# The keys' stage of a delta-rule attention: taps as diagonal matrices, blocks to lanes by DMA

## What is computed

```python
mixed = x @ W_qkv
xp = jnp.pad(mixed, ((0, 0), (KW - 1, 0), (0, 0)))
conv = sum((xp[:, i:i + Tt, :] * conv_w[:, i] for i in range(KW)))
mixed = jax.nn.silu(conv)
q, k, v = jnp.split(mixed, [KEY_DIM, 2 * KEY_DIM], axis=-1)
...
def step(S, inp):
    qt, kt, vt, gt, bt = inp
    S = S * jnp.exp(gt)[..., None, None]
    pred = jnp.einsum('bhk,bhkv->bhv', kt, S)
    u = (vt - pred) * bt[..., None]
    S = S + jnp.einsum('bhk,bhv->bhkv', kt, u)
    o = jnp.einsum('bhk,bhkv->bhv', qt, S)
    return (S, o)
```

## Time and profile before

| | us |
|---|---|
| runs timed | 5175.81, 5176.11, 5183.47, median 5176.11 |
| the profiled execution | 5175.35 |
| its span, first to last instruction | 5173.4 |
| TensorE, VectorE, ScalarE, GpSimd busy | 4783.1, 3891.6, 3016.7, 690.7 |
| keys' stage, first layer | 283.2 to 820.8 |
| keys' stage, second layer | 2819.0 to 3356.9 |

### The profile page before, as it was taken

The page is one execution under the profiler, slowest core; times in us unless marked ns, Lnnn a source line. Parts: engine busy times, 40 slices in busy tenths (PEclk is TensorE's granted clock), DMA queues, the critical chain, the costliest instruction groups (busy, mean ns, idle before and its releaser), DMA issues. The chain is left out here.

```text
span 5173.4 us, 92884 instructions
## 1 busy us (share of the span) xinstructions
PE 4783.1 (92%) x33236; PEld 4034.2 (78%) x33236; DVE 3891.6 (75%) x7782; ACT 3016.7 (58%) x9830; POOL 690.7 (13%) x740
## 2 busy tenths in 40 slices
PE   5999875999999999999969989399999999999998
PEld 3577754888888888888845877378888888888887
DVE  6837797888878878878852488877787877777876
ACT  1134544777777777777721454266666666666665
POOL 0000000221121121122100000011212111212121
PEclk7999987999999999999979999699999999999999
DMA  1022322222222222222200232222222222222222
GB/s 54 27 83 101 124 99 84 77 78 69 77 81 74 77 78 69 81 77 76 67 29 25 94 119 103 99 77 79 74 75 82 69 77 78 71 77 83 69 77 61
DMA packets 481684, 397.20 MB, mean 77 GB/s; under 512 B 302280, under 2 KB 377592, under 8 KB 480782
## 3 DMA queue, kind: packets, MB, share of 16 engines
q1 hardware_dynamic: 481230, 391.29, 25.0%
HBM read 287.79 MB, written 103.38 MB: 76 GB/s over the span
## 5 line engine op out<-in xcount | busy, mean ns | idle before, releaser
L1116 DVE SCALAR_TENSOR_TENSOR conv_l<-mix_l,taps_l,conv_l 128x512 f32<-128x512 f32 x1152 | 865.0, 751 | 271.1 <-ACT conv_l L948 243.9
L757 PE MATMUL pj_l<-x_high,w_high_l 128*128 128x512 f32 x1280 | 586.7, 458 | 159.5 <-ACT w_high_l L957 159.5
L757 PE MATMUL pj_l<-x_high,w_low_l 128*128 128x512 f32 x1280 | 512.0, 400 | 0.1
L757 PE MATMUL pj_l<-x_low,w_high_l 128*128 128x512 f32 x1280 | 512.1, 400 | 0.0
L1318 POOL TENSOR_TENSOR fac_l<-den_l,powers 128x4 f32<-128x4 f32 x256 | 257.7, 1007 | 1833.5 <-DVE den_l L1239 1830.6
L922 PE MATMUL gb_l<-wo_l,gT_l 128*128 128x256 f32 x2048 | 481.7, 384 | 0.0
L404 PE MATMUL pk_l<-x_high,wf_high_l 128*128 128x512 f32 x1024 | 425.0, 415 | 20.9 <-DVE wf_low_l L490 20.9
L1084 ACT ACTIVATE Z_l<-gb_l 128x128 f32<-128x128 f32 x1024 | 266.7, 290 | 296.9 <-PE gb_l L913 296.9
L922 PEld LDWEIGHTS gb_l<-wo_l,gT_l 128*128 128x128 f32 x2048 | 370.0, 190 | 73.9 <-ACT Z_l L1084 31.0
L1249 DVE SCALAR_TENSOR_TENSOR x<-gb_l,fac_l,x 128x256 f32<-128x256 f32 x1024 | 413.1, 476 | 10.1
L757 PEld LDWEIGHTS pj_l<-x_high,w_high_l 128*128 128x128 f32 x1280 | 241.3, 189 | 229.1 <-ACT w_high_l L957 159.8
(11 more groups left out here) (188 smaller groups left out, 10884.5 us busy)
## 6 DMA issues: line engine op xcount, KB each, us to landing
rows_l<-rows_dram SPq DMA_DIRECT2D x128, 1024.0 KB, 5.5
k_dram<-kT_l SPq DMA_DIRECT2D x128, 256.0 KB, 2.0
kk_dram<-key_kkS_l SPq DMA_DIRECT2D x128, 256.0 KB, 2.0
kq_l<-k_dram SPq DMA_DIRECT2D x128, 256.0 KB, 3.3
kkS_l<-kk_dram SPq DMA_DIRECT2D x128, 256.0 KB, 5.7
w_raw_l<-in_wx SPq DMA_DIRECT2D x32, 640.0 KB
t_dram<-lane_t_l SPq DMA_DIRECT2D x6, 1536.0 KB, 6.9
key_taps_l<-in_ktaps SPq DMA_DIRECT2D x32, 256.0 KB, 3.7
```

The source lines that it names most:

```text
L757: ins = nc.tensor.matmul(pj_bank(c, t), wt[:, k, t, :], xt[:, k, :, at], start=(k == 0 and n == 0), stop=(k == KD - 1 and n == 2))
L1116: ins = nc.vector.scalar_tensor_tensor(out, mix[:, t, :, i:i + P], wt(i), out, ALU.mult, ALU.add)
```

## The change

It rebuilds key_blocks for both layers; the other stages stay.

- TensorE projects without taps (6 products), subtracts from the sum in place the high part that ScalarE has copied out, by one product with the matrix -1, so that the low part is left (1 product), and convolves high and low parts with diagonal matrices of the taps (4 taps x 3 terms = 12 products). The four key products stay. The steps run one slot apart: project(q), subtract_high(q - 1), convolve(q - 2), products(q - 3). Sums of the projection lie in three banks pk, those of the taps in two banks pc.
- ScalarE copies the high part (keep_high) and the low part (keep_low), makes SiLU and copies the products. It makes eight 128x128 tap matrices for each head (tap_diagonals), four in each of the slots c = 2 and c = 3. Its copies into own are gone. Group work now comes six slots behind the end of a group.
- SyncE stores, besides keys and products, the diagonal blocks of each slot from kkS to own_dram, by eight DMAs of 32 x 4 x 32 elements (16 KB each), and loads them by head into lanes (load_lanes, 512 KB) once all stores of the head have landed. Taps come by one DMA at the start.
- VectorE has no folding and no transpose. It makes the low part of unfolded weights (a quarter of the size), prepares all heads of a group together, and GROUPED is (1, 2, 2, 2, 2, 2, 2, 2, 1).

The core of the diff:

```diff
-    RING = 4
-    WAITING = 5
-    GROUPED = (2, 3, 3, 3, 2, 2, 1)
+    RING = 6
+    AHEAD = 4
+    LANED = 6
+    GROUPED = (1,) + (2,) * 7 + (1,)
     MOST = max(GROUPED)
+    STORES = 1 + QUADS * GROUPS
...
+    group_of = [k for k, n in enumerate(GROUPED) for _ in range(n)]
+    behind = [CHUNKS * (last_of[k] + 1) for k in range(len(GROUPED))]
...
+        pk = ps("pk", [P, 3, WIDE])
+        pc = ps("pc", [P, 2, WIDE])
...
+                    for r in range(QUADS):
+                        rows = slice(r * QUAD, (r + 1) * QUAD)
+                        own = by4(kkS[rows, q % 2, :])[:, :, rows]
+                        for g in range(GROUPS):
+                            lane = r * QUAD + (c * GROUPS + g) * BATCH
+                            sp.dma_start(m.own_dram[L][h, lane:lane + BATCH].rearrange("b i j -> i b j"),
+                                         own).then_inc(kk_out[q % 2], 16)
+
+                def load_lanes(h):
+                    for par in range(2):
+                        sp.wait_ge(kk_out[par], 16 * STORES * (h + 1) * CHUNKS // 2)
+                    if h >= LANED:
+                        sp.wait_ge(solve, STEPS * (group_of[h - LANED] + 1))
+                    sp.dma_start(K[:, ring_of(h), :, :], m.own_dram[L][h]).then_inc(lane_in[ring_of(h)], 16)
...
+                    for k in range(1, len(GROUPED)):
+                        if q == behind[k] + 7:
+                            store_blocks(k - 1)
+                    if q < SLOTS:
+                        sp.wait_ge(k_silu, q + 1)
+                        sp.dma_start(m.k_dram[L][h, c], kT[:, q % 2, :]).then_inc(k_out[q % 2], 16)
                     if q >= 1:
                         store_products(q - 1)
+                    if q >= 1 and c == 0:
+                        load_lanes(h - 1)
...
+                    at = slice(HALO + c * P, HALO + (c + 1) * P)
+                    terms = ((wk_high, m.x_high), (wk_high, m.x_low), (wk_low, m.x_high))
+                    for k in range(KD):
+                        for n, (wt, xt) in enumerate(terms):
+                            ins = nc.tensor.matmul(pk[:, q % 3, :], wt[:, h % RING, k, :], xt[:, k, :, at],
+                                                   start=(k == 0 and n == 0), stop=(k == KD - 1 and n == 2))
+                    ins.then_inc(k_mm, 1)
...
+                    pe.wait_ge(high_ok, q + 1)
+                    nc.tensor.matmul(pk[:, q % 3, :], minus[:, :],
+                                     p_high[:, h % 2, :, HALO + c * P:HALO + (c + 1) * P], start=False, stop=True,
+                                     skip_group_check=True).then_inc(rest_mm, 1)
...
+                    pe.wait_ge(low_ok, q + 1)
+                    if c == 0:
+                        pe.wait_ge(diag_ok, 2 * TAPS * (h + 1))
+                    if q >= 2:
+                        pe.wait_ge(k_silu, q - 1)
+                    terms = ((tap_high, p_high), (tap_low, p_high), (tap_high, p_low))
+                    for i in range(TAPS):
+                        for n, (wt, pt) in enumerate(terms):
+                            ins = nc.tensor.matmul(pc[:, q % 2, :], wt[:, h % 2, i, :],
+                                                   pt[:, h % 2, :, c * P + i:(c + 1) * P + i],
+                                                   start=(i == 0 and n == 0), stop=(i == TAPS - 1 and n == 2))
+                    ins.then_inc(c_mm, 1)
...
+                for q in range(SLOTS + 3):
+                    if q < SLOTS:
+                        project(q)
+                    if 1 <= q < SLOTS + 1:
+                        subtract_high(q - 1)
+                    if 2 <= q < SLOTS + 2:
+                        convolve(q - 2)
+                    if q >= 3:
+                        products(q - 3)
...
+                    for i in some:
+                        for src, dst in ((taps_high[:, :, :].bitcast(F32), tap_high), (taps_low[:, :, :], tap_low)):
+                            nc.scalar.activation(dst[:, h % 2, i, :], eye, ACT.Copy,
+                                                 scale=src[:, h, i:i + 1]).then_inc(diag_ok, 1)
...
+                    act.wait_ge(k_mm, q + 1)
+                    if c == 0 and h >= 2:
+                        act.wait_ge(c_mm, CHUNKS * (h - 1))
+                    nc.scalar.activation(p_high[:, h % 2, :, HALO + c * P:HALO + (c + 1) * P], by4(pk[:, q % 3, :]),
+                                         ACT.Copy).then_inc(high_ok, 1)
...
+                def copy_products(q):
                     act.wait_ge(kk_mm, q + 1)
...
+                        act.wait_ge(kk_out[q % 2], 16 * STORES * (q // 2))
...
+                    if q < SLOTS:
+                        keep_high(q)
+                    if 1 <= q < SLOTS + 1:
+                        keep_low(q - 1)
+                    if 2 <= q < SLOTS + 2:
+                        silu(q - 2)
+                    if q >= 3:
+                        copy_products(q - 3)
+                    if q < AHEAD:
+                        weights_high(q + 1)
+                    if c >= 2 and h < KHEADS - 1:
+                        tap_diagonals(h + 1, range(2 * c - 4, 2 * c - 2))
+                    if q == 4:
+                        act.wait_ge(lanes_in, 16 * 2 * QUADS)
+                        spread_gains(0)
+                        spread_gains(1)
+                    for k in range(len(GROUPED) - 1):
+                        if k >= 1 and behind[k] <= q < behind[k] + GROUPED[k]:
+                            n = last_of[k - 1] + AHEAD + 1 + q - behind[k]
+                            if n < KHEADS:
+                                weights_high(n)
+                        if q == behind[k] + 6:
+                            if k >= 1:
+                                transpose_blocks(k - 1)
+                            if k + 2 < len(GROUPED):
+                                spread_gains(k + 2)
...
+                for k, size in enumerate(GROUPED):
+                    if k >= 1:
+                        for h in range(last_of[k - 1] + AHEAD + 1, min(last_of[k] + AHEAD + 1, KHEADS)):
+                            weights_low(h)
+                    for n in range(size):
+                        h = first_of[k] + n
+                        dve.wait_ge(lane_in[ring_of(h)], 16 * (h // LANED + 1))
...
+                    nc.vector.tensor_scalar(n2[:, 0:size, :], diagonal(Kk), NORM_EPS, None, ALU.add).then_inc(prep, 1)
+                    dve.wait_ge(prep, PREP * k + 1)
...
+                    nc.vector.tensor_tensor_scan(every(decay[:, 0:size, :, :]), every(gains[:, k % 2, 0:size, :, :]),
+                                                 every(diag[:, 0:size, :, :]), 0.0, ALU.mult, ALU.add).then_inc(prep, 1)
+                    dve.wait_ge(prep, PREP * k + 4)
+                    nc.vector.tensor_tensor(Kk, Kk, decay[:, 0:size, :, :], ALU.mult).then_inc(prep, 1)
...
+        m.own_dram = [nc.dram_tensor(f"own_dram{L}", (KHEADS, P, QUAD, QUAD), F32, kind="Internal").ap()
+                      for L in range(2)]
```

More of the change, by code:

```diff
@@ L360, in _ @@
                         sp.dma_start(dst, src[:, :, 1 - n:]).then_inc(lanes_in, 16)
-                for q in range(SLOTS):
+                for q in range(SLOTS + 1):
                     h, c = divmod(q, CHUNKS)
@@ L426, in copy_own @@
                     if q >= 2:
-                        act.wait_ge(kk_out[q % 2], 16 * (q // 2))
+                        act.wait_ge(kk_out[q % 2], 16 * STORES * (q // 2))
                     nc.scalar.activation(kkS[:, q % 2, :], kk[:, q % 2, :], ACT.Copy).then_inc(kk_cp, 1)
-                    by_b = kk[:, q % 2, :].rearrange("p (b n) -> p b n", b=BATCH)
-                    for r in range(QUADS):
-                        rows = slice(r * QUAD, (r + 1) * QUAD)
-                        nc.scalar.activation(own[rows, h % WAITING, c, :, :, :], bcast(by_b[rows, :, rows], 1, GROUPS),
-                                             ACT.Copy).then_inc(own_cp, 1)
@@ L475, in _ @@
-                copy_own(SLOTS - 1)
+                weights_high(0)
+                act.wait_ge(taps_in, 16)
+                nc.scalar.activation(taps_high[:, :, :], taps[:, :, :], ACT.Copy).then_inc(taps_ok, 1)
+                nc.scalar.activation(minus[:, :], eye, ACT.Copy, scale=-1.0).then_inc(minus_ok, 1)
+                act.wait_ge(taps_ok, 2)
+                tap_diagonals(0, range(TAPS))
+                act.wait_ge(cleared, 6)
+                for q in range(SLOTS + 3):
+                    h, c = divmod(q, CHUNKS)
+                    if q < SLOTS:
[4 more added lines that the diff above has]
+                        silu(q - 2)
+                    if q >= 3:
+                        copy_products(q - 3)
[17 more added lines that the diff above has]
+                                spread_gains(k + 2)
@@ new lines, in _ @@
+                nc.vector.memset(gain[:, :, :], 0.0).then_inc(cleared, 1)
+                nc.vector.memset(diag[:, :, :, :], 0.0).then_inc(cleared, 1)
```

(16 more changed lines are left out.)

221 lines of the change are left out of this document (85 added, 136 removed).

## The result

The changed kernel takes 5047.9 us (median of four runs, 5045.1 to 5050.3), the one before, on the same chip, 5176.0 (5170.4 to 5183.5): a ratio of 0.9752, 95% interval 0.9735 to 0.9768, 128 us faster. The forecast was 5026 us and lies 22 us low; the range of 4970 to 5125 holds the time. Of the two profiled spans, 5173.4 and 5048.5, the two keys' stages account for more than all of the difference: they shrank from 537.6 and 537.9 us to 470.2 and 469.3, which is 136 us, while the rest of the program took 4109.0 us instead of 4097.9. Over the eleven profiled executions of this case that rest, which is the same code in all, lies between 4097 and 4109, so these 11 us are not put down to the change.

What follows compares the result with a forecast made beforehand. SyncE's issues were taken as the bound, T = 5.85 us per slot; 94.3 + 63 T = 462.9 us per stage, 74.7 less than 537.6, so 5175.35 - 149.4 = 5026 us, range 4970 to 5125.

Steps and rivals of the forecast that it cites:

- TensorE's slot: In key_blocks, one head's chunk of 128 tokens in four batches: 19 products of 512 columns after the change, 5.38 us.
- the three added waits in a slot: TensorE's extra waits for things finished half a slot or more earlier: costed at nothing, 0.1 us per slot if each showed.
- SyncE as the bound: SyncE's in-order queue issues eight small stores per slot at 0.49 us each; 46.8 us per two-head group, 5.85 per slot.
- the sign that was named for this bound: TensorE's slots mid-stage 5.8 to 5.9 us apart if SyncE sets the pace, 5.4 to 5.6 if not.
- 63 T and the 10 us behind it: 63 slots of 5.85 us until head 14's last product is done, then 10 us until its lanes are in place.
- ScalarE's burst: Once per group, transposes, gain spreads and diagonals, about 7 us, stall TensorE about 2 us: 0.25 per slot, giving 5.63.
- Regrouping "costs 22 by itself": VectorE's substitution with groups (1, 2 x 7, 1) takes 269 us against 247, so regrouping alone costs 22 us.
- The tail: Stretch of the stage after TensorE's last product: about 64 us, against 68 before the change.
- VectorE's idle time: VectorE waits for data between groups of two heads, about 3 us each.
- D: Rival: small 128-byte writes bottleneck the DMA engines; at 84 ns each 5259 us, slower than before from 74 ns; chance 0.11.
- C: Rival: small stores issue dearer, 0.59 us as into lane_dram; 6.2 to 6.97 us per slot, 5070 to 5167 us; chance 0.18.
- B: Rival: SyncE keeps up, 5.63 down to 5.4 us per slot, stage 449 to 434.5, time 4998 to 4969 us; chance 0.23.

## Why the prediction was right, and where it was off

**TensorE's slot: right.** 5.38 was worked out, 5.37 measured; the three added waits in a slot cost nothing while nothing else is late. ScalarE's load was taken at 4.3 us a slot and is 3.6 (229.0 us over 64 slots).

**SyncE as the bound: right in kind.** It issues for 93% of the time. Doubled issues gave 9.82 a slot, halved ones 5.57, none 5.54. **Its size** was short. An issue in a slot without a large store ahead is 0.48, as taken (3.82 for eight), but after a lane load eight take 4.3 to 5.5 us. Behind the block stores it is not 3.7 us more, but for instance 2.4 + 1.8 + 0.7 = 4.9 us at 457 to 467 (2.81, 2.27 and 4.56 against 0.43, 0.43 and 3.82). A k_dram store, issued back to back, costs 0.48 with its gap, not 0.36. A group takes 50.25 us instead of 46.8. And the sign that was named for this bound, TensorE's slots 5.8 to 5.9 us apart, did not come: they are 5.4 apart, the sign named for its absence, with one long slot per group. The waits and the issues of SyncE are what tells.

**63 T and the 10 us behind it: the step that failed.** TensorE's last product for head 14 began 374.4 us into the stage and took 1.05, so it ended at 375.5, against a forecast of 6.6 + 63 x 5.85 = 375.2: T came out at 5.90 from the first product on (+3), the start at 3.9 (-2.7). That 5.90 is so near to 5.85 is in part luck: it is a mean of some 24 slots at TensorE's own 5.4, before a group's work comes in between, and of 6.4 later on. The sum had one even pace. And from there to the lanes of head 14 in place it took 18.3 us instead of 10. The rows:

```profile
660.30 1.05 PE L450 MATMUL key_kk_l<-kT_l 128*128 128x128 f32 x8
```

```profile
661.39 0.60 ACT L505 ACTIVATE key_kkS_l<-key_kk_l 128x512 f32<-128x512 f32 x1 [0.29 <-PE key_kk_l L450]
```

```profile
662.59 6.59 SPq L362 DMA_DIRECT2D own_dram<-key_kkS_l  x8
669.23 0.47 SPq L390 DMA_DIRECT2D k_dram<-kT_l  x1
669.75 0.43 SPq L356 DMA_DIRECT2D kk_dram<-key_kkS_l  x1
670.22 3.84 SPq L362 DMA_DIRECT2D own_dram<-key_kkS_l  x8
675.22 0.34 SPq L370 DMA_DIRECT2D lane_k_l<-own_dram  x1
```

The copy is done at 661.99, and SyncE comes to it at 669.75. It is 7.8 us behind, since it is still issuing the slot before, whose eight small stores took 6.59 us instead of 3.82, right behind a pair of block stores. The sum had put SyncE's pace on every slot and then let SyncE start at once on the last one. A queue that sets the pace can run behind its producers by as much as their buffers allow, and so it did here, with two buffers for the products. The lane load is in place 4.4 us after its issue began, which is the median too, where 0.5 + 2.7 were taken. The copy and the last small store's landing were 0.3 and 0.6 quicker than taken. For the stage: +0.3 up to the last product, +8.3 behind it, 42.7 against 43.8 for the last group (-1.1), 33.7 against 33.9 for the end: 470.2 against 462.9. In the second stage the miss is 6.4 us. Of the 24.5 us between the forecast's span (5024.0) and the measured one these are 13.7, and the other 11 lie in the rest of the program, whose time varies by as much between the runs.

**ScalarE's burst: right in kind, not added where it hurts.** I had taken the larger of two bounds, 5.63 with the burst and 5.85 by SyncE. The stalls of 2.9 to 6.1 us show that they meet: ScalarE has no lead because of the stores. With the issues halved mostly 1.9 us were left of it (2.0 were forecast), and with the gains spread later 0.3 at most.

**Regrouping "costs 22 by itself": wrong as time.** As VectorE's busy time it is right (19 more). As time it is a gain of 38 us a stage, 69 us of the kernel. The stretching of TensorE by VectorE's bursts stood in the text ahead of the sum, and I gave all of it to the folded weights that go. The trace of before gives 3.0 of TensorE's 25.5 us of waiting to them and 19.9 to the decay of groups of three, for which ScalarE waits in its list. (The substitution of the old groups adds up to 246 us, not 247.) The total came out near because the sum was built from the new kernel's bounds, not from differences. That is luck in part: as an account of what each part brings it was wrong twice, since the groups are a gain and the DMA part is a loss.

**The tail** was to be 64 us and is 73.5: 7.3 for the end that comes later, and 1.9 since TensorE is done earlier. **VectorE's idle time** was to be 3 us a group and is 5 to 9, by the same 3.5 us of SyncE's group.

**The rivals.** D, small writes as the bottleneck, is out. The DMA engines in a stretch of 2 us in which only small stores are under way:

```profile
q1 hardware_dynamic: 596, 0.07, 24.0%
...
own_dram<-key_kkS_l SPq DMA_DIRECT2D x5, 16.0 KB, 1.5
```

0.240 x 16 x 2 us / 596 = 12.9 ns for a write of 128 bytes, far from 74. A store of 16 KB lands after 1.5 us here, 1.6 in the median of both stages. The read-modify-write that the Trainium skill states in "DMA: Bandwidth & Descriptors", Specifications, for less than 512 bytes does not make these writes dearer than the loads of the same size, 12.6 ns. What it adds to either, no run shows. C, dearer issues by their kind, is out by 3.82 us for eight. B, SyncE keeping up, is what halving the issues makes true: 437 us a stage and 4985, inside B's 4969 to 4998.

## What to carry to other kernels

Price a move from engines to DMA by the issues it adds to its queue, about 0.48 us each here and none of them hidden once the queue is full, and merge them first: the same move cost 25 us a stage with eight stores a slot and gained 8 with four (437 against 445 us; by the ratios of the whole kernel these two can't be told apart). When a queue sets the pace, count its backlog in the sum as well as its pace, and expect the delay to appear in one piece wherever the next burst comes. In an engine's list written by hand, look for an instruction that waits for the end of a group of work: all that stands behind it waits too, and smaller groups shorten it. Undo each part of a mixed change singly: here one line, the group sizes, brought 38 of the 68 us a stage, and one part was a loss.

## What the runs showed of the hardware

- The length of an issue does not depend on the bytes of a small store: 16 stores of 8 KB took 7.5 us at the least, 8 of 16 KB 3.8.
- Issues slow down behind large stores even when another queue issued those: 5.2 to 6.0 us for eight beside GpSimd's 768 KB stores, 3.82 otherwise.
- 128-byte writes to device memory with a stride cost 12.9 ns each of a DMA engine's time, about as much as the reads of that size.
- After an idle time of 4.7 or 6.1 us TensorE's first product took 0.80 us, after 2.9 us of idling 0.50. The granted clock stood at 1.2 GHz for 6.83 us, from 441.20 and from 492.40 us on, near the end of the first two of the long idle times, and for 3.4 us from 646.00 on, 1.4 us behind the end of the short one. A slot lost about 2.5 to 3 us to the clock beside 6.1 and 4.7 us of idling (13.95 and 12.99 us against 5.37). The granted clock of the stage, 0.88, is a mean of stretches at 2.4 and at 1.2 GHz. In the kernel with twice the issues, whose TensorE idles in most slots, the stage's clock was 0.81 and the same 1728 products were busy for 429.9 us instead of 361.8, at no cost that shows: SyncE waited 2.1 us for engines in 580. In the one with halved issues and the later gains it was 0.91.
